# A first batch's norm in blocks, constants ahead of weights, and a re-dealt work plan in a fused mixer, attention and expert kernel

## What is computed

```python
xn = _layernorm(x)                                   # (8, 512, 256)
# branch 1: input product, causal convolution of 4 taps, a linear recurrence over 512 steps, silu, output product
u = conv(xn @ W_in + b_in) + conv_b
h = At @ h + u_t * Bp;  y = Cp . h + Dp * u_t         # At = tanh(A), 16 states
a = silu(y) @ W_out + b_out
# branch 2: attention, 16 heads of 16, softmax over 512 keys, with values from xn
# branch 3: 8 experts, weights of the two largest gates of a softmax over xn @ W_gate
out = x + a + attn_out + moe_out
```

## Time and profile before

| | us |
|---|---|
| median of 3 runs | 809.58 (809.55 to 812.46) |
| the profiled execution | 809.57 |
| its span, first to last instruction | 807.7 |
| busy: PE, DVE, ACT, POOL | 771.6, 588.6, 535.5, 395.1 |

### The profile page before, as it was taken

How to read it: one execution, slowest core, us unless ns; L and a number is a source line. 1 busy time by engine, 2 the same in 40 slices (tenths; PEclk the granted TensorE clock), 3 DMA queues, 4 the chain that set the end, 5 groups by cost and what they waited for, 6 DMA issues and landing times.

```text
span 807.7 us, 13231 instructions
## 1 busy us (share of the span) xinstructions
PE 771.6 (96%) x4404; PEld 450.0 (56%) x4404; DVE 588.6 (73%) x845; ACT 535.5 (66%) x926; POOL 395.1 (49%) x527
## 2 busy tenths in 40 slices
PE   9788999999999999999999999999999998999996
PEld 7555565555555665565555555566555554554553
DVE  6777976976669776997669866797658967579730
ACT  4645666666667766767667766668566766667765
POOL 7543653554335723465347633357144543435544
PEclk9899999999999999999999999999999999999999
DMA  8201101122011211103111121113111121212100
GB/s 274 61 2 41 47 22 41 40 67 63 20 30 37 83 51 41 39 2 93 40 41 41 31 81 37 37 30 93 40 41 41 28 60 30 52 31 64 34 2 26
DMA packets 32465, 39.09 MB, mean 48 GB/s; under 512 B 8513, under 2 KB 18535, under 8 KB 32398
## 3 DMA queue, kind: packets, MB, share of 16 engines
q1 hardware_dynamic: 31418, 37.29, 17.6%
q10 hardware_dynamic: 852, 0.80, 0.3%
q0 software_dynamic: 128, 0.16, 0.1%
HBM read 8.74 MB, written 4.19 MB: 16 GB/s over the span
## 4 chain that ended last, share of the span: by engine, by line
PE 80%; DVE 14%; issue 4%; ACT 2%; POOL 0%; POOLq 0%; DVEq 0%; ACTq 0%
PE PS L454 41%; PE SB L581 12%; PE PS L614 11%; DVE mx L1039 8%; PE TB L598 6%; PE PS L511 4%; PE PS L470 2%; DVE ys L889 1%; PE PS L621 1%; DVE xl L921 1%; PE PS L545 1%; PE PS L466 1%; DVE woutl L868 1%; DVE ys L885 0%; ACT Pt L821 0%
## 5 line engine op out<-in xcount | busy, mean ns | idle before, releaser
L1039 DVE TENSOR_REDUCE mx<-SB 128x2 f32<-128x1024 f32 x256 | 312.9, 1222 | 154.2 <-PE SB L581 153.3
L1102 POOL TENSOR_TENSOR acc<-acc,mt 128x256 f32<-128x256 f32 x320 | 250.5, 789 | 241.7 <-ACT mt L666 177.0
L821 ACT ACTIVATE Pt<-TB 128x1024 f32<-128x1024 f32 x251 | 257.4, 1026 | 44.6 <-PE TB L598 41.5
L666 ACT ACTIVATE mt<-PS,cpad 128x256 f32<-128x256 f32 x256 | 107.4, 470 | 85.7 <-PE PS L454 85.1
L581 PE MATMUL SB<-kst,qst 48*128 48x512 f32 x512 | 128.1, 497 | 13.1 <-DVE mx L1039 10.5
L614 PE MATMUL PS<-Pt,V 128*17 128x512 f32 x1024 | 134.7, 598 | 1.1 <-ACT Pt L821 1.1
L454 PE MATMUL PS<-weh,xTh 128*128 128x512 f32 x256 | 110.9, 433 | 2.3 <-DVE ml L897 1.2
L581 PEld LDWEIGHTS SB<-kst,qst 48*128 48x128 f32 x512 | 47.6, 183 | 110.2 <-issue 51.5
L598 PE MATMUL TB<-qst,kst 50*128 50x512 f32 x502 | 101.8, 401 | 0.8 <-ACT Pt L821 0.6
L454 PE MATMUL PS<-wel,xTh 128*128 128x512 f32 x256 | 101.2, 395 | 0.0
L454 PE MATMUL PS<-weh,xTl 128*128 128x512 f32 x256 | 100.7, 393 | 0.0
(11 more groups left out here) (162 smaller groups left out, 1161.5 us busy)
## 6 DMA issues: line engine op xcount, KB each, us to landing
qst<-qkh SPq DMA_DIRECT2D x124, 64.0 KB, 2.3
kst<-qkh SPq DMA_DIRECT2D x124, 64.0 KB, 2.2
out<-acc SPq DMA_DIRECT2D x8, 512.0 KB, 2.9
qst<-qkl SPq DMA_DIRECT2D x62, 64.0 KB, 2.2
kst<-qkl SPq DMA_DIRECT2D x62, 64.0 KB, 2.3
acc<-in_x SPq DMA_DIRECT2D x7, 512.0 KB, 3.8
Bt<-in_wexp SPq DMA_DIRECT2D x2, 512.0 KB, 8.1
raw<-in_wexp SPq DMA_DIRECT2D x2, 512.0 KB, 8.8
```

The lines of the kernel that those rows point to most:

```text
L666: return e.activation(mt[:, item % NM, :], P, ACT.Copy, scale=scale)
L821: e.activation(Pt[:, T % NP, :, :], turned_bank(T)[:, :, :], ACT.Exp, scale=0.25).then_inc(s_ex, 1)
L1039: e.tensor_reduce(mx[:, g % 2, 0:2, 4 * jj + a], SB[:, :, :], AX.X, ALU.max).then_inc(s_mx, 1)
L1102: e.tensor_tensor(v, v, mt[:, item % NM, :], ALU.add).then_inc(s_mt, 1)
```

## The change

1. The norm of batch 0 goes block by block: statistics, `ve` and power of one block, and the norm of block a-1 behind the sums of block a. The power on POOL is four instructions of one column.
2. ACT sends all four small constants of the squarings first; a dummy tanh follows, then the two real ones, and only then the DMA of the value weight. The first weight W_Q0 is sent by SP, behind the four input blocks.
3. The squarings move one place ahead: three instead of two stand ahead of T, with 3 idle turns behind each instead of 2, two more behind T, and `krylov(8)` ahead of `score(0)`. The response product stands behind the first V unit instead of the second.
4. ACT rounds the blocks of `xn` at steps -1, -1, 0, 1 (before -1, 0, 1, 2), and POOL does its four parts at steps 0, 0, 0, 1, all ahead of the expert splits.
5. In DVE's `at_start`, the bias remainder moves to step 2, `Rl` to step 3, and the split of W_IN to step 4.
6. The planner: second Qs of batch 0 from step 5 (before 7), bias units from step 6 (before 5), and no unit is added behind a Z in the same row (`break`). This deals the units anew in some 150 of 272 rows, up to step 262.

```diff
-            return max(after(("T", b, 1), 1), 32 * b - 10 if i < 2 else 32 * b + 6 if b else 7)
+            return max(after(("T", b, 1), 1), 32 * b - 10 if i < 2 else 32 * b + 6 if b else 5)
         if kind == "B":
-            return 5
+            return 6
...
-            else:
-                load(*u, t)
+                break
+            load(*u, t)
...
-KRYLOV = {("T", 1): (2, 3), ("D", 0): (4,), ("D", 1): (5,), ("D", 2): (6,), ("D", 3): (7,)}
+KRYLOV = {("T", 1): (3, 4), ("D", 0): (5,), ("D", 1): (6,), ("D", 2): (7,), ("D", 3): (8,)}
...
-            for s in range(2):
+            for s in range(3):
                 krylov(s)
-                idle_turns(2)
+                idle_turns(3)
...
-            for i in (C_BP, C_CR):
+            for i in (C_BP, C_CR, C_CC, C_D0):
                 e.dma_start(*small[i]).then_inc(s_c[i], 16)
-            e.dma_start(stages[W_Q0][0], kp_rows(wqk0)).then_inc(s_w[W_Q0], 16)
...
+            e.dma_start(stages[W_VG][0], kp_rows(wvg)).then_inc(s_w[W_VG], 16)
...
                 if t == 2:
+                    e.wait_ge(s_wh, 1)
+                    e.tensor_tensor(bst[64:68, :], bwr[64:68, :], F(bst[64:68, :]), ALU.subtract).then_inc(s_sl, 1)
+                elif t == 3:
                     e.wait_ge(s_Rh, 1)
                     e.tensor_tensor(Rl[:, :], Rraw, F(Rh[:, :]), ALU.subtract).then_inc(s_Rl, 1)
-                elif t == 3:
-                    split(W_IN)
...
-            for k in range(9):
-                layer_norm(0, k)
+            for a in range(4):
+                block_sums(0, a)
+                if a:
+                    norm(0, a - 1)
+            norm(0, 3)
...
-            e.wait_ge(s_ve, 1)
             e.wait_ge(s_hp, 1)
-            e.tensor_tensor(rs[:, :], ve[:, :], mhalf[:, :], ALU.pow).then_inc(s_rs, 1)
+            for a in range(4):
+                e.wait_ge(s_ve, a + 1)
+                e.tensor_tensor(rs[:, a:a + 1], ve[:, a:a + 1], mhalf[:, a:a + 1], ALU.pow).then_inc(s_rs, 1)
...
-                    a = t - XH[b] - 1
-                    if 0 <= a < 4:
+                    for a in (range(3) if t == 0 else (3,) if t == 1 else ()) if b == 0 else range(4):
```

## The result

| | before | after |
|---|---|---|
| median | 809.81 (809.17 to 812.46, 7 runs) | 814.93 (814.77 to 817.43, 7 runs) |
| span of the profiled execution | 807.7 | 813.0 |
| busy: PE, DVE, ACT, POOL | 771.6, 588.6, 535.5, 395.1 | 773.4, 589.1, 535.2, 393.7 |

The changed kernel is slower: ratio 1.0061, 95% interval 1.0045 to 1.0078. I had forecast 804.3 us and faster. The four engines' busy times are the same within 2 us. Of the 5.3 us by which the span grew, 3.5 are idle time of PE (36.1 us before, 39.6 after) and 1.8 are busy time of PE: the five added idle turns (1.1 by my term of 0.21 each), and products that ran at the low clock.

What follows compares the result with a forecast made beforehand. PE was taken to set the pace. Steps up to score(13) gain 7.4 us, the added idle turns included; low clock takes back 1.7 and 0.4, later steps nothing: 809.6 - 5.3 = 804.3 us, range 800.5 to 809.5.

Steps and rivals of the forecast that it cites:

- Part 6: Steps from 14 on, with units dealt anew: zero change, 3 us either way, bounded by waits for a maximum.
- Part 2: Squarings one place ahead: five more idle turns of 0.21 us on PE's path ahead of T, +1.07 us.
- Part 1: Norm by blocks and constants first, at the start: no cost, `xn` complete between 9.8 and 11.3 us, ahead of T.
- Part 3: Start of Z: `xn` parts done by 32, so `Rl` releases Z at 37.5 us instead of 38.35.
- a rule: DVE's two-input split of W_IN and POOL's split exclude each other at a shared SBUF port; split kept at 2.62 us.
- Parts 4 and 5: Steps 4 to 13: new 3.0 us hole at B, 3.60 us `xTl` wait gone, score(13) at 68.9 instead of 77.76.
- The clock: Two falls to low clock: near score(4) and Z, costing 1.7 us, and behind B0, costing 0.4 us.
- Rival 3: Re-dealt steps: DVE becomes the bound, PE pays for convolution taps, 814 us; chance 0.08.

Runs made afterwards that it cites:

- e6: The changed kernel with one unit, the first Y of batch 1, moved from row 28 to 29; 813.84 us, ratio 1.0042 to the kernel before.
- e7: The changed kernel with nine units moved by one row each; 809.67 us, ratio 0.9994 to the kernel before.
- e10: e9 with three units moved by one row; 803.11 us, ratio 0.9904 to the kernel before.
- e9: The changed kernel with its new rows up to row 27 and the old rows from 28 on; 805.85 us, ratio 0.9941 to the kernel before.
- e4: The changed kernel with squarings, idle turns and response product placed as before; 815.54 us, ratio 1.0050 to the kernel before.
- e12: The changed kernel with POOL's second expert split one step later; 812.53 us, ratio 1.0018 to the kernel before.
- e8: The changed kernel with DVE's work of steps 2 to 4 ordered as before; 815.85 us, ratio 1.0069 to the kernel before.
- e2: The kernel before with only the new planner's deal of units; 810.65 us, ratio 1.0002 to the kernel before.
- e14: The same kernel as e2, measured a second time; 810.86 us, ratio 1.0003 to the kernel before.
- e5: The changed kernel itself, measured again beside other runs; 815.96 us, ratio 1.0066 to the kernel before.

## Why the prediction was wrong, point by point

**Part 6 failed**, and with it the sign. I put the re-dealt steps at zero, 3 us either way, on the ground that the units are the same, that 49 rows instead of 48 are without a large unit, and that a wait for a maximum is 0.9 us. From step 20 to the end they lost 10.7 us. The excess in single steps grew by 8.6 us: 5.6 of them are waits for a bank, with the low clock behind one of them, and 2.4 are waits for a maximum. The bound was made from one kind of wait, the score's for a maximum, and from the row of the weight loads, 51.0 us in 54 times, where PE's own row has 10.5 in 19. The kind that I had in my own list for the front, a unit that waits for its bank, I did not look for behind it: no row of the kernel before that I had chosen showed it, though its step 40 was the pattern X, T, T, M. The planner's costs know PE and DVE time by row and nothing of the bank that the fourth unit of a row needs. The proof is in the runs that keep the units and change only their rows: units moved by one row take back 2.1 us (e6), 6.3 (e7) and 2.7 (e10), and with the old rows from 28 on (e9) the time is 1.2% below that of the changed kernel.

**Part 2 was right in mechanism.** From the first squaring to score(1) the kernel before took 26.64 - 8.47 = 18.17 us, the changed one 26.51 - 7.59 = 18.92: 0.75 more, where I had 1.07 less the 0.24 that I left out. But the first squaring came 0.88 us earlier, which I had ruled out. That is no merit of the change: it began anywhere from 7.02 to 8.53 us in the profiled executions of both codes. And by e4's trace the term was worth nothing in this kernel, since PE waits for DVE ahead of score(4) in any case. Part 1 cost nothing, as said: a power of one column took 0.65 us, between my two bounds, and `xn` was complete at 10.13, ahead of T at 10.82.

**Part 3 had the right releaser and a wrong term.** Z waited for `Rl`, but started at 38.69 instead of 37.5, later than before. The term was the bias remainder, 1.10 us: it took 3.66. I had taken its price from the row of before, where it stood beside a short split, and did not ask what POOL would be doing at its new place. What I weighed against a rule was the split of W_IN, kept at 2.62; that one took 1.23 us at 40.74, and POOL's third expert split, issued 0.04 us behind it, took 3.41 instead of 2.35. By the Trainium skill, page "SBUF — State Buffer", section "Who interferes with whom", the order of issue decides which of the two engines has the port, for the whole of its instruction. By that rule, the trace agrees (1.23 and 3.41 there; in e12 the remainder ended 0.55 us behind POOL's running split); the trace differs from it in the changed kernel, where the remainder was issued at 32.48, ahead of the second split (33.26), and still waited for it; there the measurement decides. I had leaned on the rule and applied it to the wrong instruction.

**Parts 4 and 5 were right in mechanism, and too early.** B waited 2.54 us for `qkl` (3.0 forecast), V of batch 1 followed Y with no wait, and score(13) came at 72.60, outside the 69 to 71 that I had named as the sign. That is 5.2 us earlier than before; I had 68.9. Of the 3.7 us too many, 1.2 came with score(4), 1.6 more by score(7), which started at 53.04 where I had 50.3, and the rest by score(9), with Y at low clock from 53.8 us. **The clock:** two falls at the places named. The second I had put at 0.4 us, since it would lie over waits; it lay over Y, which took 2.56 us to the next score where the next Y took 1.49 to the V unit behind it. I did not foresee the third, behind the wait at step 28.

**Rival 3** (slower, since DVE becomes the bound in the re-dealt steps; chance 0.08) came nearest. It put the price in taps behind maxima; the larger part was banks (5.6 us of excess against 2.4). It deserved more than the chance of a mishap, since nothing that I had read bounded the new rows from above.

## What to carry to other kernels

When a change re-deals a schedule, list the rows of the new order, not only their count: look for units that need a buffer whose reader stands behind this step's longest instruction on another engine, and price each at its wait. A gain at the front is easily lost in new rows behind it, so cut the new and the old order at a row where both have done the same work, and take each half from the better one. Price an instruction by what the neighbouring engine does at its new place, not by its old row.

## What the runs showed of the hardware

- A DVE instruction with two inputs in SBUF was held until POOL's two queued splits were both over, and ended 0.55 to 0.68 us behind them: 3.84 us for one of 0.83 in e8, 3.66 for one of 0.68 in the changed kernel. With one split, in e12, it took 1.35. That the second split of POOL can go ahead of a DVE instruction that has been waiting since the first was new to me. It doesn't always: in the kernel before, DVE's waiting split of W_IN went ahead of POOL's next instruction.
- PE's 16 idle turns at the start took 5.44 us in e2 and 6.75 in e14, which are one kernel. That moved score(4) by 0.9 us (34.03 and 34.93), but score(12) by only 0.3 (69.05 and 69.32).
- One further stretch of low clock cost 1.1 us. The changed kernel and e5 are one kernel, and both waited 1.50 us for the maximum ahead of score(214), at 677.35 and 677.19. Behind it the clock fell in e5 and not in the other, and e5 lost 1.1 us more in the next three steps; e2 and e14, again one kernel, differ by the same amount at the same place. The window 675 to 680 us in e5:

```profile
675.00:680.00 5.00, 3.50 (x18) 1.71 (x10) 4.74 (x13) 1.79 (x2) 1.85 (x6) 0.85 0.01 3
```

The same in the changed kernel:

```profile
675.00:680.00 5.00, 3.20 (x20) 1.37 (x12) 4.74 (x13) 2.25 (x3) 1.86 (x6) 1.00 0.02 4
```
